# Filling the expert lists inside the batch loop, a ring of eight result rows, a last pass with four buffers, and other engine orders in a four-layer transformer kernel

## The reference

```
x = x + LN(window_and_latent_attention(LN(x)))
x = x + LN(ternary_ffn(LN(x)))                 # 256 -> 1024 -> 256, exact gelu
x = x + LN(rwkv6(LN(x)))                       # a recurrence over 512 steps, 16 heads of 16
x = x + LN(experts(LN(x)))                     # 16 experts, the best 4 of each token, and a shared one
```

## Time and profile before

| | before |
|---|---|
| median of 3 runs | 2776.1 us (2770.41 to 2780.48) |
| the profiled execution | 2776.92 us |
| its span, first to last instruction | 2775.1 us |
| mean granted clock of PE | 0.84 |
| PE, DVE, ACT, POOL busy | 69%, 57%, 31%, 29% of the span |
| start, until the first activation | 0 to 252 us |
| attention of batch 0 alone | 252 to 441 us |
| woven loop (7 x 206 us) and recurrence of batch 7 | 441 to 2029 us |
| routing | 2035 to 2255 us |
| tile groups (18) | 2257 to 2651 us |
| last pass | 2651 to 2775 us |

### The profile page before, as it was taken

How to read it: one execution, slowest core, us unless ns; L and a number is a source line. 1 busy time by engine, 2 the same in 40 slices (tenths; PEclk the granted TensorE clock), 3 DMA queues, 4 the chain that set the end, 5 groups by cost and what they waited for, 6 DMA issues and landing times. The chain is left out here.

```text
span 2775.1 us, 34488 instructions
## 1 busy us (share of the span) xinstructions
PE 1927.4 (69%) x10658; PEld 1206.9 (43%) x10659; DVE 1572.6 (57%) x3248; ACT 847.5 (31%) x1771; POOL 792.1 (29%) x627
## 2 busy tenths in 40 slices
PE   0003879978988988989979979976534446677665
PEld 0001545544544544544544544542134436666532
DVE  0201245966966966966966966966645534444433
ACT  0001334433433433433533523521023313333300
POOL 0000000431431431431431431432437733333310
PEclk9655679999999999999998998986566668878988
DMA  9996000000000000000000000000034423333345
GB/s 330 328 324 221 1 8 1 1 9 9 1 8 9 1 8 9 1 11 6 1 16 1 1 16 1 1 8 0 0 104 155 143 97 99 103 98 96 99 167 197
DMA packets 140821, 186.75 MB, mean 67 GB/s; under 512 B 12089, under 2 KB 127485, under 8 KB 140544
## 3 DMA queue, kind: packets, MB, share of 16 engines
q10 hardware_dynamic: 69104, 78.79, 8.9%
q1 hardware_dynamic: 58512, 70.32, 8.1%
q0 software_dynamic: 13056, 35.68, 3.3%
HBM read 65.06 MB, written 121.78 MB: 67 GB/s over the span
## 5 line engine op out<-in xcount | busy, mean ns | idle before, releaser
L562 DVE TENSOR_TENSOR_SCAN s_buf<-r_work,kvb 128x512 f32<-128x512 f32 x256 | 362.2, 1415 | 0.0
L662 POOL TENSOR_TENSOR p_buf<-s_buf,r_work 128x512 f32<-128x512 f32 x128 | 151.7, 1185 | 486.9 <-DVE s_buf L562 486.9
L662 POOL TENSOR_TENSOR r_work<-s_buf,r_work 128x512 f32<-128x512 f32 x128 | 165.0, 1289 | 228.7 <-DVE s_buf L562 228.7
L1567 POOL DMA_INDIRECT y_rows<-m_ys,m_y_idx x144 | 141.0, 979 | 262.3 <-ACT m_ys L1643 164.7
L722 ACT ACTIVATE probs<-bank_s,nmx 128x256 f32<-128x256 f32 (+1 forms) x512 | 187.0, 451 | 93.6 <-DVE nmx L425 90.0
L740 ACT ACTIVATE pt<-bank_s 128x1024 f32<-128x1024 f32 (+1 forms) x128 | 117.5, 918 | 250.0 <-PE bank_s L1001 250.0
L551 DVE TENSOR_TENSOR kvb<-r_work,bank 128x512 f32<-128x512 f32 x256 | 174.5, 682 | 24.4 <-PE bank L1119 14.0
L856 PE MATMUL bank_s<-xT,wqkv 128*128 128x512 f32 x128 | 63.6, 645 | 168.0 <-ACT xT L691 168.0
L425 DVE TENSOR_REDUCE nmx<-bank_s 128x4 f32<-128x1024 f32 (+1 forms) x128 | 138.2, 1080 | 63.4 <-PE bank_s L951 62.7
L627 POOL TENSOR_TENSOR rstd<-vare,mhalf 128x4 f32<-128x4 f32 x48 | 48.3, 1007 | 432.5 <-DVE vare L358 432.5
L1118 PE MATMUL bank<-v_hi,sel_v 128*128 128x512 f32 x256 | 137.7, 538 | 22.7 <-DVE kvb L551 14.8
(11 more groups left out here) (322 smaller groups left out, 4350.1 us busy)
## 6 DMA issues: line engine op xcount, KB each, us to landing
x_rows<-empty_row ACTq DMA_DIRECT2D x16, 4608.0 KB, 35.1
m_xs<-x_rows SPq DMA_DIRECT2D x146, 144.0 KB
w_lo<-y_rows SPq DMA_DIRECT2D x8, 2048.0 KB
m_x_tok<-x_after_rwkv SPq DMA_DIRECT2D x10, 512.0 KB
w_raw<-in_w SPq DMA_DIRECT2D x17, 256.0 KB
x_new<-in_x SPq DMA_DIRECT2D x8, 512.0 KB, 3.5
x_after_rwkv<-x_b SPq DMA_DIRECT2D x8, 512.0 KB, 3.7
out<-m_x_tok SPq DMA_DIRECT2D x8, 512.0 KB, 2.8
```

What stands on the lines that cost most here:

```text
L562: V.tensor_tensor_scan(s_buf[:, n % 2, 1:S + 1], dec[:, n // HD, :], kvb[:, n % 2, :], 0.0, ALU.mult, ALU.add).then_inc(sem["state"], 1)
L662: G.tensor_tensor(p_slot(n), s_buf[:, n % 2, 0:S], rf[:, n // HD, :], ALU.mult).then_inc(sem["rs"], 1)
L1567: G.indirect_dma_start(y_rows, bass.IndirectOffsetOnAxis(y_idx[:, u % Y_RING:u % Y_RING + 1], 0), ys[:, u % Y_RING, :], None, bounds_check ...
```

## The change

There are four edits. The fills of `x_rows` leave ACT: SP issues eight pieces of 9.4 MB, `empty_rows(b)`, the first behind `next_x(0)`, six in SP's loop between `next_x(b)` and `store(b-1)`, and the eighth with the 128 last rows behind the loop; SP waits for them at its end. `Y_RING` is 8, and the memory of `ys` is shared with `w_raw`, into which the weights are loaded before the tiles. The last pass has four buffers for `y4` (in `w_lo` and `w_hi`) and four for x; the x of the first four batches is loaded behind the last L1483, ahead of the waits for the scatters. All four order strings are different.

```diff
-    vector="arararrrrarrraaraarrrrrararararrararrararrarraararrararararraararraarrararaaararararrrarrrararaaarraaraaraaaaaraa",
+    vector="ararrrarrarrraararrrrraarraararrarararraarrarararrarraarrararararraarraarrarararaarrrrararraararraaaaraaraaaaaraa",
...
+            def empty_rows(b):
+                n = N_ROWS // B
+                sp.dma_start(x_rows[bass.ds(b * n, n)].rearrange("(r p) c -> p r c", p=P),
+                             empty_row[:].unsqueeze(1).broadcast_to([P, n // P, ROW])).then_inc(rows_empty, 16)
+
             sp.dma_start(x_new[:], rows(t["x"][0:1])).then_inc(sem["x_in"], 16)
             next_x(0)
+            sp.wait_ge(rows_made, 1)
+            empty_rows(0)
             with sp.Fori(1, B - 1) as b:
                 next_x(b)
+                empty_rows(b)
                 store(b - 1)
+            empty_rows(B - 1)
+            sp.dma_start(x_rows[N_ROWS:N_ROWS + P], empty_row[:]).then_inc(rows_empty, 16)
             store(B - 2)
             store(B - 1)
+            sp.wait_ge(rows_empty, 16 * (B + 1))
...
-            sc.wait_ge(rows_made, 1)
-            for e in range(NE):
-                sc.dma_start(x_rows[e * B * S:(e + 1) * B * S].rearrange("(r p) c -> p r c", p=P),
-                             empty_row[:].unsqueeze(1).broadcast_to([P, B * S // P, ROW])).then_inc(rows_empty, 16)
-            sc.dma_start(x_rows[N_ROWS:N_ROWS + P], empty_row[:]).then_inc(rows_empty, 16)
             sc.wait_ge(const_ready, 1)
...
-Y_RING = 4
+Y_RING = 8
...
-        w_raw = sb("w_raw", [P, 2, WE])
+        w_in_ys = sb("w_in_ys", [P, Y_RING * D])
+        w_raw = w_in_ys[:, 0:2 * WE].rearrange("p (a c) -> p a c", c=WE)
...
-        ys = sb("m_ys", [P, Y_RING, D])
+        ys = w_in_ys[:].rearrange("p (a d) -> p a d", d=D)
...
+        RING = 4
...
+            sp.wait_ge(sem["h_f"], at(B, "h_f", 0) + TILES)
+            for b in range(RING):
+                load_x(b)
             for u in range(Y_RING):
                 sp.wait_ge(ys_out[u], 16 * TILES // Y_RING)
-            for b in range(2):
+            for b in range(RING):
                 load_y(b)
             for b in range(B):
                 sp.wait_ge(sem["x_final"], b + 1)
-                sp.dma_start(rows(out[b:b + 1]), x_tok[b % 2][:]).then_inc(sem["x_out"], 16)
-                if b + 2 < B:
+                sp.dma_start(rows(out[b:b + 1]), x_end[b % RING]).then_inc(sem["x_out"], 16)
+                if b + RING < B:
                     sp.wait_ge(sem["x_out"], 16 * (b + 1))
-                    load_y(b + 2)
+                    load_x(b + RING)
+                    load_y(b + RING)
```

## The result

The changed kernel takes 2464.2 us (median of 4 runs, 2458.2 to 2467.3), beside 2773.3 us for the kernel before in the same comparison (4 runs, 2764.7 to 2780.5): 0.888 of the time, interval 0.885 to 0.892. The prediction was 2509, with a range from 2468 to 2560. The direction and three of the terms held; the time lies 45 us under the forecast and 4 us under the range. The profiled execution took 2467.3 us, with a span of 2465.5.

The account below looks back on a forecast made before the run. The prediction took ACT's queue of fills, scatter waits, last-pass load waits and a nearly full woven loop as bounds: 2776.9 - 191 (start) - 60 (ring) - 37 (last pass) + 20 (orders) = 2508.9, so 2509 us, range 2468 to 2560.

Parts of the forecast that it names:

- The start: Up to ACT's first activation: with the fills off ACT's queue, L691 starts at 60.2 us instead of 251.8, -191 us.
- The fills in the loop: Woven loop: each 29 us piece ends before the next store matters, so 0 us (0 to +30).
- The last pass: Final pass: four batches in flight end the waits for loads and PE is the bound, -37 us (-25 to -42).
- The orders: New order strings in the woven loop: 2.9 us more per iteration, +20 us over seven (-15 to +55).
- The rest: Woven loop outside FFN and gate: same work on a saturated DVE, a gain of 1 at L568 and no other.
- The FFN's cost: FFN in the loop: 16 fillers move behind the wait, 3.75 us, plus 1.65 for a possible half clock, per iteration.
- The gate's gain: Before the gate: the last scan no longer waits behind DVE's wait for PE, so L1017 comes 2.5 us sooner per iteration.
- The ring of eight: Tile groups: with eight slots the wait for the `y_rows` scatter ends, -60 us (-40 to -80).
- That is 18.2: Length of a tile group: 4.18 register loads, 6.21 to the third tile's turn, 7.8 for further tiles; 18.2 us against 21.9.
- the orders gain: Rival for the woven loop: FFN waits are covered by DVE and the gate gains 2.5 x 7; 2471 us, chance 0.22.
- a stall that moves: Rival for the tile groups: POOL or the PE, ACT, DVE chain takes over, -60 becomes nearly 0; 2569 us, chance 0.07.
- a fill paid in the loop: Rival for SP's queue and DMA rings: pieces delay iterations; 2738 us in full, 2544 at 5 us each, chance 0.08.

Follow-up runs that it names:

- a second piece: The changed kernel with another 9.4 MB piece after each piece in SP's loop, into a tensor nothing reads: 2501.6 us, ratio 0.903.
- -37 alone on chip A: The kernel before with only the last pass changed, to four buffers: 2742.9 us, ratio 0.987.
- strings alone (chip B): The kernel before with only the four new order strings: 2766.9 us over 10 runs, ratio 0.998.
- the ring's kernel on chip A: The kernel before with Y_RING = 8 alone and the weights' buffer in the ring's memory: 2734.3 us, ratio 0.983.
- fills by SP (A): The kernel before with only the fills moved to SP piece by piece: 2595.7 us, ratio 0.935.
- old orders (A): The changed kernel with the four old order strings, on chip A: 2512.8 us, ratio 0.905.
- old orders (E): The changed kernel with the four old order strings, on chip E: 2475.4 us, ratio 0.894.
- changed kernel (E): The changed kernel, unaltered, run again on chip E: 2467.0 us, ratio 0.890.

## Why the prediction was right or wrong

**The start: right, -186 for -191.** The 27.2 us from the last constant to the end of the turns came out at 65.06 - 37.9 = 27.2 (PE's turns start at 63.15 and take 1.91). The constants took 37.9 instead of the 33 assumed, which is 4.9 of the 5.4 that are missing. The other 0.5 is from the turns' end to the first activation at 65.59: ACT begins a table load of 1.28 us only once PE has released it, and the sum left that load out.

**The fills in the loop: right, 0.** Shown by the kernel that has none in the loop (2464.4), and by the loops on chip A, which are as long with the pieces as without. The cover is the distance from the piece's end (409.20 + 31.7 = 440.9) to the next `store` (445.34); a second piece overruns it and costs 5.5 us per iteration. The guess that SP's issue is held for the length of the transfer was wrong where one piece is in the queue (0.41 us), and right for the second (24.53).

**The last pass: right, -34 for -37**, and -37 alone on chip A.

**The orders: +20 was forecast, and they brought about -4.** The step that failed is "*The rest* has the same work in another order on a saturated DVE; I see a gain of 1 where L568 no longer stands behind the gate's three operations, and no other"; even that 1 isn't in the sum (3.75 + 1.65 - 2.5 = 2.9). The two places that the prediction worked out came as it said, and the gain that turns the sum is in a third. The mean of the second to the seventh iteration, in four stretches between the same events in both timelines (us):

| stretch | before | changed kernel | change | forecast |
|---|---|---|---|---|
| `x_free` to the end of the last FFN matmul | 31.3 | 36.5 | +5.2 | +5.4 |
| from there to the first scan | 56.9 | 57.2 | +0.3 | 0 |
| first scan to the start of the last but one | 89.1 | 85.8 | -3.3 | 0 |
| from there to the next `x_free` | 29.0 | 26.1 | -2.9 | -2.5 |
| iteration | 206.3 | 205.6 | -0.7 | +2.9 |

With the strings alone (chip B) the changed side is 36.5, 57.2, 86.1 and 26.1.

*The FFN's cost is real*, and putting the old FFN order back brings 33 us. *The gate's gain is real too.* It shows as the last scan, which no longer stands behind DVE's wait for PE. Before, and then in the changed kernel:

```profile
1186.04 1.22 DVE L562 TENSOR_TENSOR_SCAN s_buf<-r_work,kvb 128x512 f32<-128x512 f32 x1
1189.40 0.26 DVE L434 RECIPROCAL rinv<-bank 128x16 f32<-128x16 f32 x1 [2.14 <-PE bank L972]
...
1190.24 1.21 DVE L562 TENSOR_TENSOR_SCAN s_buf<-r_work,kvb 128x512 f32<-128x512 f32 x1
```

```profile
584.10 2.33 DVE L573 TENSOR_TENSOR_SCAN s_buf<-r_work,kvb 128x512 f32<-128x512 f32 x2
587.45 0.26 DVE L445 RECIPROCAL rinv<-bank 128x16 f32<-128x16 f32 x1 [1.01 <-PE bank L977]
```

The last two scans take 5.4 us from the start of the first to the end of the second before and 2.3 after, and from there to `x_free` it is 22.6 to 24.2 us before and 23.8 after.

*The scans are the third place*, and DVE was not saturated there. The stretch from the first to the last scan of one iteration, in the kernel before and in the changed one (length, then busy time of PE, PE's weight loads, DVE, ACT and POOL, PE's clock):

```profile
1096.40:1191.40 95.00, 85.69 (x676) 50.52 (x674) 85.08 (x96) 41.07 (x87) 40.87 (x32) 0.93 0.00 1
```

```profile
499.60:586.40 86.80, 80.80 (x676) 48.54 (x676) 83.20 (x92) 40.88 (x87) 38.86 (x32) 0.98 0.00 1
```

This pair is 8.2 us shorter, with the same scans. 3.1 of it is the last scan's move; the rest lies inside. DVE is idle 3.6 us in it instead of 9.9, it holds four instructions fewer, and PE's clock is 0.98 instead of 0.93. Some 2 us of the mean gain of 3.3 inside are won ahead of the first L425 (L436 after), which starts 16.9 us behind the first scan before and 14.9 after, and they are DVE's waits for PE: it is idle 3.8 us there before and 1.7 after. Before, and then in the changed kernel:

```profile
1108.87 1.29 DVE L442 TENSOR_TENSOR work<-bank_s,routb 128x512 f32<-128x512 f32 x2 [1.55 <-PE bank_s L984]
...
1114.41 0.69 DVE L425 TENSOR_REDUCE nmx<-bank_s 128x4 f32<-128x512 f32 x1 [2.53 <-PE bank_s L951]
```

```profile
511.07 1.29 DVE L453 TENSOR_TENSOR work<-bank_s,routb 128x512 f32<-128x512 f32 x2 [0.88 <-PE bank_s L989]
```

So the mistake was to take DVE's share of busy time, 85.08 of 95, as full, and to look at no place inside the scans. Over all, the seven kernels with the four old strings take 1805 to 1814 us from the first activation to the first scatter of `x_rows`, 1809.0 in the mean, and the seven with the four new ones 1800 to 1810, 1804.8 in the mean (chips mixed). That is -4, as the two medians on chip B have it, and hardly told from none.

**The ring of eight: right in kind, wrong in size, -80 for -60.** The wait for `y_rows` is gone and the register gap is 4.2 as before. The heads of the groups, L1756 and L1773 with their gap, lie (2626.40 - 2278.43) / 16 = 21.75 us apart before and (2356.25 - 2080.73) / 16 = 17.22 after, so the term to blame is "That is 18.2". Of its three parts the gap (4.2) and the tiles behind the third (7.0 to the last L1780, and a tile's end) are as said. The middle one is not: "from there to the third tile's turn at half clock, 2435.41 - 2429.20 = 6.21" was read in one group. Over the groups that distance is 4.9 to 6.3 us before, 5.5 in the mean; after, it is 4.9 to 5.2 in all but the first. The half clock at the head does stay, but the group that was chosen was one of the longest. With eight slots on chip A it is still 4.9 to 6.4, 5.7 in the mean, so the 5.0 is not the ring's doing alone. A group is 4.5 us shorter instead of 3.7, which makes 14 of the missing 20 over 17 groups; the last group, for which the forecast took 3 off, gained 3 instead and makes the other 6.

**But how much the ring brings depends on the chip, and this was not in the prediction.** On chip A it was -45, on chip B groups of 384.4 with four slots (the strings alone) stand beside 302.6 with eight, -82. With four slots the groups take 381 to 385 on either kind of chip; my reading, which no run tests, is that the wait for the scatter hides it when PE's result is late too. With eight, a tile's chain is what counts: from the third L1764 (L1780 in the changed kernel) of a group to the last are 7.9 to 8.9 us in the ring's kernel on chip A, where the changed kernel has 7.0. The profile of before that the prediction was read from has the routing of 208 us that goes with the long kind; the result came from the other. On chips of the long kind the changed kernel with a harmless instruction more took 2504.5 to 2511.5, and there 2509 would have been right, by errors that cancel (the orders said to cost 20, the ring to bring 60 where it brings 45 there). On the other kind both errors show, together with routing's 7. The lower end of the range had room for a gain by the orders or for a larger one by the ring, but not for both, and routing besides.

The rival "the orders gain", 2471, gave the nearest number, half by luck: the gate does gain, but the FFN, which it let be covered, costs 5 us per iteration, and what makes up for it are the scans, which it didn't name. The rivals of a stall that moves and of a fill paid in the loop didn't come.

## What to carry to other kernels

An engine that is busy 90% of a stretch need not be saturated: here 3.3 us of 89 were to be had. Before an order is judged by the two places where its rows are seen to move, take the whole iteration in stretches, write down each engine's idle time in each, and let an order reach for all of it; then put back the part that costs (here the FFN's, which gives 2431.7 us).

A long transfer ahead of a short one on the same queue was free here where it ended before the short one was issued, and cost 5.5 us per iteration where it ended some 20 us later; work out that distance before moving one there.

Compare a variant with its twin on the same chip, stage by stage. A difference in a stage that the edit doesn't reach may be the chip's; run the same kernel on both chips before any of it is explained.

## What the runs showed of the hardware that was not expected

The chips fall into two kinds for this kernel. On A, C and D routing takes 206 to 209 us and the groups with eight slots 335 to 338; on B and E, and in the result, 201 and 302 to 305. The stages ahead of the routing don't show it in any kernel, and the kernel with the old strings, which ran on A and E, had a mean granted clock of 0.858 and 0.870. In the groups with eight slots PE is also busy longer on the long kind, and at a lower granted clock, 0.85 against 0.90. The ring's kernel on A and the changed kernel:

```profile
2269.00:2605.00 336.00, 248.41 (x1693) 234.37 (x1691) 167.72 (x637) 132.32 (x495) 138.99 (x142) 0.85 0.37 110
```

```profile
2071.00:2373.00 302.00, 227.34 (x1690) 223.27 (x1689) 166.66 (x637) 130.12 (x494) 139.96 (x143) 0.90 0.41 125
```

That is 21 of the 34 us. Whether late results keep the clock down or the clock makes them late isn't shown; the three results above were late, or on time, at a clock of 1.00.

1740 matmuls of the program raise a semaphore. With each rise in the trace put to the last matmul that ended before it, so many rises come over 0.3 us behind the end of their matmul, and so many matmuls are left without a rise:

```
                       over 0.3 us late    without a rise
before (its profile)          25              119
fills by SP (A)               19              124
ring of eight (A)            140              141
old orders (A)               125              150
old orders (E)                 0                1
orders only (B)                0                8
changed kernel                 0                1
changed kernel (E)             0                2
```

All late ones lie in the routing and the expert part. Most are late by 0.3 to 2 us. Since rises are missing from the traces of the long chips, some that count as late may belong to another matmul, so the counts are rough and no sum of the delays is given; the times of the runs don't depend on that. On the long chips the kernels with eight slots have five to seven times as many as those with four. What makes a result late on one chip and not on another is open: no edit here turned it on or off, and it was seen only as far as the trace shows the semaphore.

A second thing: the granted clock at the gate is not what sets its length. In the kernel with only the new strings PE stands 1.2 us ahead of L1134 in each of the seven iterations; in the 7 us behind, the clock is 0.56 in most and 1.00 in two, and L1017 starts 12.3 us behind the last scan's end in all of them.
